# Attention contexts of two halves in one go: pairs of column-tiled products, eight tiles of probabilities, and late scores through one PSUM bank

## The reference, cut to what matters

```python
q = lora(x, Wq, Aq, Bq)          # 32 heads of 32
k = lora(ctx, Wk, Ak, Bk)        # 8 heads of 32, each for 4 query heads
v = lora(ctx, Wv, Av, Bv)
scores = einsum('bhqd,bhtd->bhqt', q, k) / sqrt(32)
attn = softmax(scores, axis=-1)
context = einsum('bhqt,bhtd->bhqd', attn, v)
out = x + lora(context, Wo, Ao, Bo)
```

## Time and profile before

| | |
|---|---|
| median of 3 runs | 1350.19 us (1350.06 to 1354.49) |
| the profiled execution | 1352.2 us, span 1350.4 us |
| granted clock over the span, mean | 0.997 |
| PE busy | 98% of the span |
| DVE, ACT, POOL busy | 69%, 61%, 12% |
| stage of layer 0 | 0 to 398.4 us |
| query projections with early scores | 398.4 to 880.7 us |
| pairs 0 to 15 | 880.7 to 1350.4 us |

### The profile page before, as it was taken

How to read it: one execution, slowest core, us unless ns; L and a number is a source line. 1 busy time by engine, 2 the same in 40 slices (tenths; PEclk the granted TensorE clock), 3 DMA queues, 4 the chain that set the end, 5 groups by cost and what they waited for, 6 DMA issues and landing times.

```text
span 1350.4 us, 23739 instructions
## 1 busy us (share of the span) xinstructions
PE 1326.5 (98%) x7135; PEld 1051.9 (78%) x7135; DVE 929.8 (69%) x2075; ACT 827.7 (61%) x2931; POOL 160.7 (12%) x129
## 2 busy tenths in 40 slices
PE   6999999999999999999999999999999999999999
PEld 4778888888888888888888888766767676766666
DVE  5666666666665777777777776586776777666666
ACT  4566666555550777777757776766566666665441
POOL 6533333222210000000000001400000000000000
PEclk9999999999999999999999999999999999999999
DMA  6455556667756888788777888989998999988872
GB/s 186 149 187 196 195 193 197 223 222 223 233 177 195 247 236 232 216 234 231 229 212 218 236 230 266 278 243 246 262 247 235 256 249 254 252 235 230 235 226 87
DMA packets 194817, 300.42 MB, mean 222 GB/s; under 512 B 26562, under 2 KB 93732, under 8 KB 194180
## 3 DMA queue, kind: packets, MB, share of 16 engines
q1 hardware_dynamic: 194692, 298.90, 76.6%
HBM read 213.88 MB, written 84.93 MB: 221 GB/s over the span
## 4 chain that ended last, share of the span: by engine, by line
PE 94%; DVE 2%; DMA 1%; ACT 1%; SPq 1%; issue 1%; DVEq 0%; ACTq 0%
PE bank L669 25%; PE bank L711 23%; PE bank L562 13%; PE bank L730 7%; PE bank L763 5%; PE bank L774 5%; PE bank L622 3%; PE bank L544 2%; PE bank L507 2%; PE bank L640 2%; PE bank L587 1%; PE bank L655 1%; PE bank L592 1%; PE bank L524 1%; PE bank L604 1%
## 5 line engine op out<-in xcount | busy, mean ns | idle before, releaser
L981 ACT ACTIVATE bank<-bank,negs 128x128 f32<-128x128 f32 x1024 | 347.2, 339 | 188.1 <-DVE negs L1236 187.7
L669 PE MATMUL bank<-hT,wq 128*128 128x512 f32 x1488 | 390.4, 400 | 0.0
L711 PE MATMUL bank<-wo,op 128*128 128x512 f32 x1344 | 345.7, 394 | 1.2 <-issue 1.2
L669 PEld LDWEIGHTS bank<-hT,wq 128*128 128x128 f32 x1488 | 263.9, 189 | 46.1
L711 PEld LDWEIGHTS bank<-wo,op 128*128 128x128 f32 x1344 | 249.0, 188 | 53.0 <-issue 2.4
L1231 DVE TENSOR_REDUCE maxes<-bank 128x4 f32<-128x512 f32 x256 | 175.5, 685 | 117.3 <-PE bank L730 116.9
L998 ACT ACTIVATE probT<-bank 128x512 f32<-128x512 f32 x256 | 151.2, 602 | 103.9 <-PE bank L763 101.4
L981 ACT ACTIVATION_READ_ACCUMULATOR bank<-bank,negs 128x1 f32 x1024 | 208.4, 204 | 0.0
L562 PE MATMUL bank<-wkv_hi,yT 128*128 128x512 f32 x512 | 201.5, 421 | 0.0
L730 PEld LDWEIGHTS bank<-k_stack,q_stack 96*128 96x128 f32 x1024 | 150.4, 191 | 16.3 <-issue 0.6
L730 PE MATMUL bank<-k_stack,q_stack 96*128 96x128 f32 x1024 | 147.3, 266 | 0.4 <-DMA q_stack<-q_dram 0.4
(11 more groups left out here) (167 smaller groups left out, 1634.6 us busy)
## 6 DMA issues: line engine op xcount, KB each, us to landing
q_stack<-q_dram SPq DMA_DIRECT2D x256, 256.0 KB, 4.0
q_dram<-q_part SPq DMA_DIRECT2D x64, 512.0 KB, 4.2
q_stack<-q_dram SPq DMA_DIRECT2D x256, 128.0 KB, 4.3
y_in<-in_ctx SPq DMA_DIRECT2D x32, 512.0 KB, 4.4
x_in<-in_x SPq DMA_DIRECT2D x32, 512.0 KB, 5.2
h_dram<-h_out SPq DMA_DIRECT2D x32, 512.0 KB, 2.6
h_in<-h_dram SPq DMA_DIRECT2D x32, 512.0 KB, 3.7
k_stack<-k_dram SPq DMA_DIRECT2D x128, 128.0 KB, 3.4
```

The costliest lines, as they stand in the source:

```text
L669: m = pe.matmul(bank(u % 2).rearrange("p (a n) -> p a n", a=2), wq[:, block, part, c, :], hT[(group + 1) % 2][:, :, of, c, :], start=c == ...
L711: mm = pe.matmul(out_bank(pair, m), op[m][:, of, c, :], wo[m][w][:, c, :], start=c == 0 and of == 0 and w == 0, stop=c == GROUP - 1 and of ...
L981: act.activation(part, part, ACT.Exp, bias=negs[:, n % RING, j:j + 1], scale=SCORE1, accum_out=sums[:, score_column(k), g, j:j + 1]).then_ ...
```

## The change

From half 2 on, contexts are made two halves at a time: eight matmuls one behind the other, the even half into bank 3 and the odd into bank 7, in slot -3 of the lead-in and in slots 5 and 13 of pairs 0 to 14 (31 of them; halves 0 and 1 stay alone). The probabilities get eight tiles instead of five, two of them in the score's query stack, one in the first query buffer. The late scores keep bank 6 alone, at slots 0, 3, 6, 10 and 13, and SP loads their queries one unit at a time. Splits 0 and 1 of the next pair move from slots 5 and 9 to 7 and 8; the logarithm's steps in pairs 5 and 11 (4 and 11 before) come a slot earlier within the pair. There are now 7 late scores in the lead-in and 53 in pairs 0 to 10; in pair 5 they leave out slots 3 and 6.

The diff, cut to what the prediction speaks of:

```diff
-        PROBS = 5
-        probT = sb("probT", [P, PROBS, BANK])
+        probT = [sb(f"probT{i}", [P, BANK]) for i in range(5)]
...
+        q_spare = at[0]
...
+        for place in (stack_place + 2 * 4 * BANK, stack_place + 3 * 4 * BANK, q_spare):
+            at[0] = place
+            probT.append(sb(f"probT{len(probT)}", [P, BANK]))
...
             elif w < QUERY_SLOTS:
-                take = w % 3 == 0
+                take = QUERY_SLOTS - w in (22, 19, 16, 13, 10, 7, 3)
             else:
-                take = i in (1, 5, 7, 10, 13) and (i > 9 or pair not in log_steps)
+                take = i in (0, 3, 6, 10, 13) and (i not in (3, 6) or pair not in log_steps)
...
-        context_at = {QUERY_SLOTS - AHEAD + GQ * k + 5: k for k in range(HALVES)}
+        context_at = {QUERY_SLOTS - AHEAD + GQ * k + 5: (k,) for k in range(2)}
+        context_at |= {QUERY_SLOTS - AHEAD + GQ * k + 8: (k, k + 1) for k in range(2, HALVES, 2)}
...
+        for n in range(HALVES * GQ):
+            i = n % 7 if n < 8 else (1, 2, 3, 7, 4, 5, 6, 0)[n % 8]
+            prob_tile[n] = probT[i]
+            prob_freed[n] = last_in[i] // GQ + 1 if i in last_in else 0
+            last_in[i] = n
+        LAST_TILE_FIRST = next(n for n in prob_tile if prob_tile[n] is probT[7])
+
+        def context_bank(k):
+            return bank(3 + 4 * (k % 2))
...
-            return bank(5 + n % 3 if score_slot[n] < LAST_EARLY else 6 + n % 2)
+            return bank(5 + n % 3 if score_slot[n] < LAST_EARLY else 6)
...
-                pe.wait_ge(S["st_exp"], GQ * (k + 1))
-                for g in range(GQ):
-                    m = pe.matmul(bank(3)[g * HD:(g + 1) * HD, :], v_in[:, k % 2, g, :],
-                                  probT[:, (GQ * k + g) % PROBS, :], start=True, stop=True)
-                m.then_inc(S["pv_mm"], 1)
+                pe.wait_ge(S["st_exp"], GQ * (last + 1))
+                for k in halves:
+                    for g in range(GQ):
+                        m = pe.matmul(context_bank(k)[g * HD:(g + 1) * HD, :], v_in[:, k % 2, g, :],
+                                      prob_tile[GQ * k + g][:], start=True, stop=True)
+                    m.then_inc(S["pv_mm"], 1)
...
-                if n >= PROBS:
-                    act.wait_ge(S["pv_mm"], (n - PROBS) // GQ + 1)
+                if prob_freed[n]:
+                    act.wait_ge(S["pv_mm"], prob_freed[n])
+                elif n == LAST_TILE_FIRST:
+
+                    act.wait_ge(S["q_out0"], 2 * DMA * NC * NG // 4)
...
-                    if i == 5:
+                    if i == 7:
                         split_op(pair + 1, 0)
-                    if i == 9:
+                    if i == 8:
                         split_op(pair + 1, 1)
...
-            def load_stack(stack, k, g, done):
+            def load_stack(stack, first, k, g, heads, done):
...
+                heads = 1 if n >= TWO_STACKS else 2
```

More of the change, by code:

```diff
@@ L165, in xattn_two_layers @@
         negs = sb("negs", [P, RING, GQ])
+        assert at[0] <= end
+        at[0] = sums_place
+        lse_rows = sb("lse_rows", [P, 1, 2, P])
         at[0] = last_place
@@ L348, in log_chunk @@
         def log_chunk(w, after):
-            return log_at.get(w - after)
+            first, last = log_at.get(w - after), log_at.get(w - after + (after != LOG_ADD))
+            return first if first is not None and first < 2 else last if last is not None and last >= 2 else None
         def again_slot(n):
@@ L389, in xattn_two_layers @@
         for n in range(SCORE_UNITS):
-            where = 5 + n % 3 if n < EARLY_SCORES else 6 + n % 2
+            where = 5 + n % 3 if n < EARLY_SCORES else 6
             score_freed[n] = last_in.get(where, -1) + 1
@@ L406, in xattn_two_layers @@
         BLOCK_DONE = (2, 10, 8, 11)
-        FIRST_STACK_LAST = LAST_EARLY - 4
-        score_place, place_freed = {}, {}
-        last_in = {}
+        TWO_STACKS = EARLY_SCORES
+        assert TWO_STACKS % 2 == 0
+        score_place, place_freed, score_source = {}, {}, {}
+        last_in, loads = {}, {}
         for n in range(SCORE_UNITS):
[L414 to L421, removed]
+            place = n % 8 if n < TWO_STACKS else n % 2
+            score_place[n] = place
+            place_freed[n] = last_in.get(place, -1) + 1
+            last_in[place] = n
+            if n >= TWO_STACKS or n % 2 == 0:
+                source = f"score_one{place}" if n >= TWO_STACKS else f"score_in{place // 2}"
+                loads[source] = loads.get(source, 0) + 1
+                score_source[n] = source, 2 * DMA * loads[source]
         def again_stack(k):
@@ L444, in xattn_two_layers @@
         soonest = 0
-        for n in range(0, SCORE_UNITS, 2):
+        for n in score_source:
             soonest = max(soonest, 8 * queries_out(score_half(n)) + 12)
-            if place_freed[n + 1]:
-                soonest = max(soonest, score_slot[place_freed[n + 1] - 1] + 1)
+            freed = place_freed[n if n >= TWO_STACKS else n + 1]
+            if freed:
+                soonest = max(soonest, score_slot[freed - 1] + 1)
             score_load_at.setdefault(soonest, []).append(n)
@@ L738, in turn_log @@
                 if chunk >= 2:
-                    pe.wait_ge(S["c"], sum(w <= log_slot[chunk] + LOG_TURN for w in context_at))
+                    pe.wait_ge(S["c"], sum(len(of) for w, of in context_at.items() if w < log_slot[chunk] + LOG_TURN))
                 elif chunk:
@@ L765, in scores_again, with contexts @@
                           start=True, stop=True).then_inc(S["st_mm"], 1)
[L767 to L770, removed]
[L771 to L776 removed]
+            def contexts(halves, w):
+                last = halves[-1]
+                for k in halves:
+                    pe.wait_ge(S[f"v_in{k % 2}"], DMA * (k // 2 + 1))
+                if last >= 2:
+                    pe.wait_ge(S["c"], last - 1)
+                pe.wait_ge(S["lse_lo"], sum(slot + LOG_ROWS <= w for slot in log_slot.values()))
+                pe.wait_ge(S["st_exp"], GQ * (last + 1))
+                for k in halves:
+                    for g in range(GQ):
+                        m = pe.matmul(context_bank(k)[g * HD:(g + 1) * HD, :], v_in[:, k % 2, g, :],
+                                      prob_tile[GQ * k + g][:], start=True, stop=True)
+                    m.then_inc(S["pv_mm"], 1)
             turn_y(0)
@@ L847, in tensor_program @@
                 if w in context_at:
-                    context(context_at[w], w)
+                    contexts(context_at[w], w)
                 for n in again_at.get(w, ()):
@@ L1010, in evacuate_context @@
                 act.wait_ge(S["pv_mm"], k + 1)
-                act.copy(c_sb[:, k % 4, :], bank(3)).then_inc(S["c"], 1)
+                act.copy(c_sb[:, k % 4, :], context_bank(k)).then_inc(S["c"], 1)
             def keep_product(pair):
@@ L1067, in scalar_program @@
                     probabilities(n)
-                if w - 1 in context_at:
-                    evacuate_context(context_at[w - 1])
+                for k in context_at.get(w - 1, ()):
+                    evacuate_context(k)
                 pair, i = step_of(w)
```

41 lines of the change are left out of this document (27 added, 14 removed).

## The result

The changed kernel takes 1396.12 us (median of 4 runs, 1395.27 to 1396.65), the kernel before, run beside it, 1351.97 (median of 4, 1350.06 to 1354.49): 1.0325 times as long, 95% interval 1.0302 to 1.0347. The forecast was 1381 with a range to 1392: the direction was right, the loss is 44 us where 31 were forecast.

What follows compares the result with a forecast made beforehand. The prediction took TensorE (PE), busy 98% of the span, as the bound. Terms -9.0 + 20.7 + 3 + 7.2 + 8.8 gave +30.7, so 1381 us for the median; range 1363 to 1392.

Steps and rivals of the forecast that it cites:

- Contexts in pairs: 31 pairs replace 62 single contexts; each second context saves 0.29 us of entry and exit: -9.0 us, ends 0 and -11.
- Slot 5 of nine regular pairs: PE waits 2.30 us for ACT's probabilities before slot 5's context, in nine pairs: +20.7 us, ends 17 and 24.
- Eight tiles: Lead-in: probability 11 waits for a query write, so L763 number 13 waits 5.9 us: +7.2 once, ends 3 and 9.
- The 1.3 for number 14: Lead-in: ACT's backlog behind probability 11 delays probability 12, holding L763 number 14 about 1.3 us more.
- Pair 0: Same chain as slot 5 plus weight casts and splits, against some 4 us waited before: +3 us, ends 0 and 7.
- The clock: Half-speed stretches behind about five of eleven PE waits, 1.75 us lost each: +8.8 us, ends 0 and 19.
- The first end: Low end of the clock term, 0: pair 0's idles of about 1 us before brought no half-speed stretch.
- Rival 2: The clock falls to half speed behind each of eleven waits: 1391 us, chance 0.08.
- PEclk below 9: Sign of the clock term: this reading in a few of the profile page's 40 slices from 870 on.
- Late scores one by one: One-unit query loads add about 3 us of SP's queue per 16 slots, covered by SP's idle: 0, end +6.
- rival 5: SP falls behind and stacks come late by up to 3 us in ten pairs: some 1390 us, chance 0.08.

Runs made afterwards that it cites:

- the two kernels with one DMA: The kernel with three repairs plus both halves' values in one DMA from half 4 on: 1342.59 us; the same with L800 between a pair's contexts: 1347.99 us.
- the run with the wait filled: Changed kernel with nine products, results overwritten, ahead of the contexts of slot 5 in the nine regular pairs: 1384.27 us (1.0246).
- the run with five products: Changed kernel with five products, results overwritten, ahead of the contexts of slot 5 in the nine regular pairs: 1384.51 us (1.0240).
- The experiment on before: Kernel before, with only the late scores' queries loaded one unit at a time into two places: 1364.14 us (1.0082).
- the two runs with one wait of the lead-in mended: Changed kernel with values of halves 0 and 1 loaded in their old slots: 1385.83 us; changed kernel with halves 2 and 3 as single contexts: 1386.16 us.
- the kernel with three repairs: Changed kernel with values' old slots, halves 2 and 3 as single contexts, and slot 3's exponentials behind slot 4's probabilities on ACT: 1349.37 us (0.9991).

## Why the prediction missed its range

**Right.** *Contexts in pairs*, -9.0: -10, 0.33 each; the two kernels with one DMA show 0.32 for one pairing (2.43 against 2.75) and 0.26 in the regular pairs. The Trainium skill (TensorEngine Tiling (Array Packing), Key Properties) has it that changing the tile within a mode costs no drain; the trace agrees: sixteen matmuls in 1.85, four waves with one entry and exit, and a second entry and exit cost 0.32. *Slot 5 of nine regular pairs*, +20.7: +20, place, number, releaser and chain as told, and undoing either end of the chain removes it. *Eight tiles*, +7.2: 5.55. The 1.3 for number 14 did not come: the product ahead of it ran at half speed, and PE reached it at 883.85, when probability 12 (882.85 to 883.47) was done. *Pair 0*, +3: +4.

**The first failed step is the one that isn't there.** The prediction puts the values of the contexts at nothing, without a word: their load slots stood in the diff's `values_at`, and I went through scores, tiles and stacks and past this line. The trace has 5.1 of wait, once, and half speed behind it; putting the slots back gave 10.

**The second is the size of *The clock*, +8.8.** The mechanism held: the run with the wait filled shows that 12 us of the regular pairs are half speed, and that idle time brings it. The term took five stretches of 3.5 us; the trace has nine, four of them 6.8 us long, which cost 3.0 instead of 1.65: +20. "About half" was a number between two ends and not one from a row. The first end, that idles of 1 us in pair 0 brought none, was true of idles of 1 us, as the run with five products shows, but the waits to come were of 2 to 6 us. Rival 2, half speed behind each wait, was nearer, and no upper bound either, since it priced all at 3.5 us. The Trainium skill (TensorE: Matmul & The Clock Gate, HAM oscillation — how this bites in real kernels) tells of a kernel that starts slow behind each of its waits, which are of some 3 to 5 us; the prediction carried that over to all eleven waits, nine of them shorter. Here it holds for the waits of 3.9 to 5.6 us, for six of nine of 2.1, and for none of 1. The sign that I named for it, PEclk below 9 in the page's slices, can't show it: a slice is 35 us long, and 6.8 us at half speed in it leave it at 0.90.

With these two, 5.1 and 11, with 1.7 less for number 13, 1 less each for the pairings and for slot 5, 1 more for pair 0, and the 2 of layer 0 off, the sum of 31 becomes some 42, with 43 between the spans and 44 between the medians.

***Late scores one by one*, 0, was right for the wrong reason.** I set the loads against SP's idle time before. The experiment on before shows that this idle time doesn't hide them all (7 us in pairs 0 to 10 there). What hid them in the changed kernel are the very waits of slot 5: pairs that are 1.5 to 4.5 longer. With the waits gone SP was late in six pairs, and rival 5 took 5.0 us in pairs 1 to 10; with two issues less a pair they came back, and 6.8 over the kernel. So the change's gain was real, 0.26 to 0.33 a pairing where nothing is late, and it was lost three times over: to two orders of instructions, to the clock behind them, and, these mended, to SP's queue.

That the half-speed stretches come behind some waits of 2.1 and not behind others of the same length is shown; what chooses among them was not tried.

## What to carry to other kernels

A wait on the matrix engine costs its length and can cost the clock behind it: price a stretch at half speed from rows, behind each wait of 2 us and more, and shorten or fill the wait first, since 1 us left idle here cost no clock. When a change rewrites a formula of slots, evaluate it before and after for every engine's list, loads included, and not for those that the change is about. And a queue's spare time belongs to the time of the kernel that was measured: count issues per period against the period that you hope for.

## What was not expected of the hardware

Nine waits of the same length, 2.10 to 2.11, at the same place of their pairs, brought half speed in six pairs of the changed kernel and in five in each of the two runs with one wait of the lead-in mended, and not in the same pairs. A stretch at half speed lasted 3.4, 6.8 or 10.2 us, the last at the first context's wait of 5 in four of the other runs and in pair 0 of one. And SP's queue was full without the DMA engines showing it: over pairs 1 to 10 their share is 0.90 in the kernel with three repairs and 0.94 in the kernel before, where SP idled 46 us. Two issues less a pair, of 0.43 us each (SP's first row above), were worth 6.8 us over the kernel.
